# Two tiles at a time in self-attention, other orders in cross attention, and a last addition in two parts

## What is computed

```python
x = x + xattn(layernorm(x), ctx, mask)     # x 32x32x1024, ctx 32x257x1024: scores against the
                                           # context itself, softmax, weighted sum of the context
x = x + attn(layernorm(x), Wq, Wk, Wv, Wo) # 16 heads of 64, causal over the 32 positions of a batch row
x = x + ffn(x, w_gate, w_up, w_down)       # silu(x @ w_gate.T) * (x @ w_up.T), then @ w_down.T; 4096 hidden
```

## Time and profile before

| | us |
|---|---|
| median of 3 runs | 1494.79 |
| lowest, highest | 1493.11, 1496.1 |
| the profiled execution | 1494.51 |
| its span, first to last instruction | 1492.7 |
| PE busy | 1471.3 |
| POOL, DVE, ACT busy | 870.1, 764.6, 550.3 |
| one looped group of self-attention | 100.87 |
| one chunk of the feed-forward loop | 57.47 |

### The profile page before, as it was taken

How to read it: one execution, slowest core, us unless ns; L and a number is a source line. 1 busy time by engine, 2 the same in 40 slices (tenths; PEclk the granted TensorE clock), 3 DMA queues, 4 the chain that set the end, 5 groups by cost and what they waited for, 6 DMA issues and landing times.

```text
span 1492.7 us, 23122 instructions
## 1 busy us (share of the span) xinstructions
PE 1471.3 (99%) x7940; PEld 1197.3 (80%) x7940; DVE 764.6 (51%) x1229; ACT 550.3 (37%) x1090; POOL 870.1 (58%) x709
## 2 busy tenths in 40 slices
PE   7899999999999999999999999999999999999998
PEld 5666888887888888888888888888888888888886
DVE  4777154162361587843634625626626526436446
ACT  4457232132231354334334334344343433443442
POOL 1224211302212121579779789789788798798795
PEclk9999999999999999999999999999999999999999
DMA  9895200101101000112112111121121121121123
GB/s 380 336 382 212 113 29 29 56 28 56 56 27 58 1 1 22 38 51 74 35 56 64 44 61 56 49 63 50 56 63 49 55 65 49 42 77 30 55 63 112
DMA packets 43382, 117.35 MB, mean 79 GB/s; under 512 B 4944, under 2 KB 5200, under 8 KB 40528
## 3 DMA queue, kind: packets, MB, share of 16 engines
q1 hardware_dynamic: 42912, 116.44, 22.4%
q10 hardware_dynamic: 432, 0.39, 0.1%
HBM read 112.62 MB, written 4.19 MB: 78 GB/s over the span
## 4 chain that ended last, share of the span: by engine, by line
PE 94%; DVE 3%; DMA 1%; issue 1%; ACT 1%; SPq 0%; POOL 0%; DVEq 0%; ACTq 0%; POOLq 0%
PE ps L1318 38%; PE ps L1338 18%; PE ps L968 9%; PE ps L970 9%; PE ps L969 9%; PE ps L1005 3%; PE ps L1026 2%; PE ps L1048 2%; PE ps L974 1%; PE ps L1119 1%; PE ps L1162 1%; DMA cT<-in_turned 1%; DVE x L1745 1%; DMA ctx<-in_ctx 0%; DVE att L1531 0%
## 5 line engine op out<-in xcount | busy, mean ns | idle before, releaser
L583 POOL TENSOR_TENSOR b_lo<-blk,b_hi 128x512 fp32r<-128x512 f32 x180 | 231.8, 1296 | 49.2 <-ACT b_hi L863 38.9
L1745 DVE TENSOR_TENSOR x<-ps,x 128x1024 f32<-128x1024 f32 x210 | 242.1, 1210 | 0.0
L494 POOL TENSOR_TENSOR w_lo<-raw,w_hi 128x2048 fp32r<-128x2048 f32 x16 | 73.6, 4600 | 274.9 <-ACT w_hi L705 274.9
L1318 PE MATMUL ps<-xT_hi,b_hi 128*128 128x512 f32 x480 | 186.7, 389 | 0.0
L1318 PE MATMUL ps<-xT_lo,b_hi 128*128 128x512 f32 x480 | 186.7, 389 | 0.0
L1318 PE MATMUL ps<-xT_hi,b_lo 128*128 128x512 f32 x480 | 186.7, 389 | 0.0
L1338 PE MATMUL ps<-b_hi,b_hi 128*128 128x512 f32 x420 | 166.4, 396 | 0.0
L1338 PE MATMUL ps<-b_lo,b_hi 128*128 128x512 f32 x420 | 163.7, 390 | 0.0
L1338 PE MATMUL ps<-b_hi,b_lo 128*128 128x512 f32 x420 | 163.5, 389 | 0.0
L1719 DVE TENSOR_TENSOR hid<-ps,kept 128x512 f32<-128x512 f32 x60 | 41.5, 692 | 233.7 <-PE ps L1318 193.8
L583 POOL TENSOR_TENSOR b_lo<-s_sum,b_hi 128x512 fp32r<-128x512 f32 x105 | 136.4, 1299 | 35.8 <-ACT b_hi L863 35.8
(11 more groups left out here) (155 smaller groups left out, 3206.9 us busy)
## 6 DMA issues: line engine op xcount, KB each, us to landing
blk<-in_blocks SPq DMA_DIRECT2D x180, 256.0 KB, 2.7
ctx<-in_ctx SPq DMA_DIRECT2D x64, 512.0 KB, 10.7
raw<-in_w SPq DMA_DIRECT2D x19, 1024.0 KB, 4.8
x<-in_x SPq DMA_DIRECT2D x8, 512.0 KB, 7.0
ext_row<-in_ext SPq DMA_DIRECT2D x8, 512.0 KB, 14.7
out<-x SPq DMA_DIRECT2D x16, 256.0 KB, 2.6
cT<-in_turned SPq DMA_DIRECT2D x3, 1032.0 KB, 9.4
mask<-in_mask ACTq DMA_DIRECT2D x1, 224.9 KB, 6.2
```

Source lines behind the costliest of these rows:

```text
L494: pool.tensor_tensor(w_lo[wslot][:, :], raw[slot][:, :], w_hi[wslot][:, :].bitcast(F32), ALU.subtract).then_inc(split_done[slot], 1)
L583: pool.tensor_tensor(b_lo[slot][:, :], src[:, :], b_hi[slot][:, :].bitcast(F32), ALU.subtract).then_inc(block_lo, 1)
L1318: mm = pe.matmul(ps[:, bank, :], stat[a], moving[b], start=first and m == 0, stop=(s == 3 and m == 2), skip_group_check=True)
L1745: dve.tensor_tensor(part, ps[:, bank:bank + 2, :], part, ALU.add).then_inc(down_added, 1)
```

## The change

It has these parts:

- Groups 0 to 2: values, scores and attend are issued for two tiles at a time, the odd tile in the upper half of the bank (`tile_cols`); values of tiles 2 and 3 go to bank 2. ACT, DVE: one instruction for both tiles where one can be (copies, maximum, reciprocal, product, transposes, low parts), with buffers of two tiles in one tensor, and `oT` for four tiles. The projections of odd tiles go to banks 2 and 3.
- All four groups: the wait for `k_kept` stands ahead of the first values; DVE adds both halves of a projection in one instruction; `wo_done` and `wo_free` count in twos. The last group keeps its order, with tile t in the half `t % 2`.
- Start: x's tile 0 is issued after one context block; PE makes 12 transposes of the identity before the first context.
- Tile 1: DVE's copy for `context(1, 3)` moves ahead of `next_normalise(2)`.
- Last tiles: the turn of tile 7 goes to banks 2 and 3, with the waits that these need; `row_hi(3)` on ACT moves behind the last probabilities, `add_readout(7)` on DVE ahead of `row_lo(4)`, `turn_rows(6)` on PE behind the first query job.
- Feed-forward: the last addition of a chunk (place 6, second half) is made in two instructions of one tile, the first as soon as its own matmuls are done (`third_done`).

```diff
@@ cross attention, SP, ACT
             for b in range(BT):
                 context(0, 0, b).then_inc(first_full[0][b], 16)
-            sync.dma_start(x[:, 0, :], x_in[:, 0, :]).then_inc(x_full[0], 16)
+                if b == 0:
+                    sync.dma_start(x[:, 0, :], x_in[:, 0, :]).then_inc(x_full[0], 16)
...
             exps(NT - 1)
-            row_hi(3)
             probabilities(NT - 1)
             weigh_extra(NT - 1)
+            row_hi(3)
+            row_normalise(5)
             row_hi(4)
-            row_normalise(5)
             row_normalise(6)
@@ cross attention, PE, DVE
             def next_turn(t):
                 pe.wait_ge(next_ready, t + 1)
-                if t > 1:
+                if t == NT - 1:
+                    pe.wait_ge(c_act_done, act_before(t * KP))
+                    pe.wait_ge(c_dve_done, dve_before(t * KP))
+                elif t > 1:
                     pe.wait_ge(readout_free, t - 1)
-                if t == NT - 1:
-                    pe.wait_ge(xt_ready, 1)
-                turn(xn[0], RO).then_inc(next_psum, 1)
+                turn(xn[0], next_bank(t)).then_inc(next_psum, 1)
...
+            for i in range(WARM):
+                pe.transpose(ps[:, SC, 0:P], ident[:, :], ident[:, :])
             context(0, 0)
...
             job(Q_BANKS[0], 0, 0).then_inc(q_done, 1)
+            turn_rows(6)
             turn_rows(7)
...
                 if t + 2 < NT:
                     next_stats(t + 2)
+                    if t == 0:
+                        context(1, 3)
                     next_normalise(t + 2)
                 add_readout(t)
                 row_stats(t)
-                context(t + 1, 3)
+                if t:
+                    context(t + 1, 3)
...
             row_lo(3)
+            add_readout(NT - 1)
             row_lo(4)
-            add_readout(NT - 1)
@@ self-attention, PE, groups 0 to 2
+                pe.wait_ge(k_kept, g * 4 + 4)
+                if not last:
...
+                    def scores_pair(i):
+                        if i:
+                            pe.wait_ge(att_read, g * 8 + 2 * i)
+                        scores(g, 2 * i)
+                        scores(g, 2 * i + 1).then_inc(att_done, 2)
...
+                    def project_tile(t):
+                        if t == 0:
+                            pe.wait_ge(split_done[3], g + 1)
+                        pe.wait_ge(oT_ready, g * 8 + 2 * (t // 2 + 1))
+                        if t == 1:
+                            pe.wait_ge(v_kept, g * 8 + 4)
+                        elif t > 1:
+                            pe.wait_ge(wo_free, g * 16 + 2 * t)
+                        project(t, PROJECT_BANKS[t % 2])
+
+                    values_pair(0)
+                    scores_pair(0)
+                    values_pair(1)
+                    values_pair(2)
+                    scores_pair(1)
+                    attend_pair(0)
+                    values_pair(3)
+                    project_tile(0)
+                    scores_pair(2)
+                    attend_pair(1)
+                    project_tile(1)
+                    project_tile(2)
+                    project_tile(3)
+                    scores_pair(3)
+                    attend_pair(2)
+                    pe.wait_ge(att_read, (g + 1) * 8)
+                    pe.wait_ge(split_done[0], g + 2)
+                    job(0, 0, 0).then_inc(q_done, 1)
+                    project_tile(4)
+                    project_tile(5)
+                    attend_pair(3)
+                    job(1, 0, 1).then_inc(q_done, 1)
+                    project_tile(6)
+                    project_tile(7)
+                    return
@@ self-attention, ACT, groups 0 to 2
+                    keep_values_pair(0)
+                    exps_pair(0)
+                    keep_values_pair(1)
+                    keep_values_pair(2)
+                    keep_heads_pair(0)
+                    exps_pair(1)
+                    keep_values_pair(3)
+                    pair_split(g, 4)
+                    keep_heads_pair(1)
+                    exps_pair(2)
+                    keep_heads_pair(2)
+                    exps_pair(3)
+                    keep_queries(g + 1, 0)
+                    keep_heads_pair(3)
+                    keep_queries(g + 1, 1)
@@ self-attention, DVE, groups 0 to 2
+            def add_projected(g, t, bank=6):
+                dve.wait_ge(wo_done, g * 16 + 2 * (t + 1))
+                part = x[:, t, :].rearrange("p (e n) -> p e n", e=2)
+                dve.tensor_tensor(part, ps[:, bank:bank + 2, :], part, ALU.add).then_inc(wo_free, 2)
...
+                    for i in range(4):
+                        if i == 2:
+                            add_tile(0)
+                        mask_tile(2 * i)
+                        if i:
+                            heads_lo_pair(i - 1)
+                        mask_tile(2 * i + 1)
+                        tops_pair(i)
+                        if i == 2:
+                            add_tile(1)
+                        if i == 3:
+                            add_tile(3)
+                        turn_pair(i)
+                        if i == 2:
+                            add_tile(2)
+                    add_tile(4)
+                    add_tile(5)
+                    heads_lo_pair(3)
+                    add_tile(6)
+                    add_tile(7)
@@ feed-forward, DVE
+                if place == 6 and q == 1:
+                    half, col = ADD_TO[place]
+                    for i in (2, 3):
+                        if i == 2:
+                            dve.wait_ge(third_done, c)
+                        else:
+                            dve.wait_ge(pair_done, c * PAIRS)
+                        part = x[:, half * 4 + i, col * HALF:(col + 1) * HALF]
+                        dve.tensor_tensor(part, ps[:, DOWN_BANKS[place] + i, :], part, ALU.add)\
+                            .then_inc(down_added, 1)
+                    return
```

More of the change, by code:

```diff
@@ new lines, in attend, with project @@
+                def attend(t):
+                    for h in range(HG):
+                        r = slice((h % 2) * DK, (h % 2 + 1) * DK)
+                        at = t % 2 * FT * P + h // 2 * P
+                        mm = pe.matmul(ps[r, 4, at:at + P], v[:, t, h * DK:(h + 1) * DK],
+                                       att_z[t % 2][:, (h % 2) * 2 + h // 2, :], start=True, stop=True)
+                    return mm
+                def project(t, bank):
+                    for f in range(FT):
+                        for half in range(2):
+                            at = f * D + half * HALF
+                            mm = three(ps[:, bank + half, :], (oT_hi[t][:, f, :], oT_lo[t][:, f, :]),
+                                       (w_hi[1][:, at:at + HALF], w_lo[1][:, at:at + HALF]),
+                                       start=(f == 0), stop=(f == FT - 1))
+                    mm.then_inc(wo_done, 2)
@@ L1146, in values, with scores_one, attend_one @@
                         pe.wait_ge(v_kept, g * 8 + t)
-                    for k in range(KD):
-                        mm = three(ps[:, 5, 0:W], tokens(k, t * P, P),
-                                   (w_hi[0][:, k * W:(k + 1) * W], w_lo[0][:, k * W:(k + 1) * W]),
-                                   start=(k == 0), stop=(k == KD - 1))
-                    mm.then_inc(v_done, 1)
-                def attend(t):
+                    values(t, 5).then_inc(v_done, 1)
+                def scores_one(st):
+                    if st:
+                        pe.wait_ge(att_read, g * 8 + st)
+                    scores(g, st).then_inc(att_done, 1)
+                def attend_one(t):
                     pe.wait_ge(att_turned, g * 8 + (t + 1))
@@ L1159, in attend, with project_one @@
                         pe.wait_ge(oT_ready, g * 8 + t)
[L1160 to L1166 removed]
+                    attend(t).then_inc(pv_done, 1)
+                def project_one(t):
                     if t == 0:
@@ L1178, in project @@
-                    mm.then_inc(wo_done, 1)
-                values(0)
-                pe.wait_ge(k_kept, g * 4 + 4)
-                scores(g, 0)
-                values(1)
+                    pe.wait_ge(wo_free, g * 16 + (2 * t + 2))
+                    project(t, 6)
+                values_one(0)
+                scores_one(0)
+                values_one(1)
                 for st in range(1, NT):
-                    pe.wait_ge(att_read, g * 8 + st)
-                    scores(g, st)
+                    scores_one(st)
@@ L1190, in group @@
                     if st >= 2:
-                        attend(WITH_SCORES[st])
+                        attend_one(WITH_SCORES[st])
                     if st < NT - 1:
-                        values(st + 1)
+                        values_one(st + 1)
                     if st == 3:
-                        attend(2)
+                        attend_one(2)
                     if st >= 2:
```

(4 more changed lines are left out.)

274 lines of the change are left out of this document (160 added, 114 removed).

## The result

The kernel before takes 1494.79 us (the median of five executions, not of three as the table ahead has it), the changed kernel 1499.4 us (median of 5, 1497.44 to 1502.31): 1.0039 times as long, with a 95% interval of 1.0027 to 1.005. It is slower. The forecast was 1494.8 and no change; the time lies inside the range, near its high end, and the direction is missed. One later execution of the kernel before took 2229.89 at a granted clock of 0.616, and is in no ratio here.

A forecast was written before the change was run, and what follows sets the result against it. PE, busy 99% of the span, was taken as the bound. Terms -4.5 + 1.0 + 0 + 2.65 + 0.9 + 0 = +0.05 on the profiled 1494.51; with the median 0.28 above it, 1494.8. Range 1491.8 to 1500.0.

The forecast's parts named there:

- start: Kernel start: x issued earlier makes context row 3 land 1.3 later; loss taken as 1.0, 0.8 if warm-up brings full clock.
- cross attention, tile 1: Earlier DVE copy for batch row 3 shortens PE's 3.79 wait and half clock: -4.5, bounds -3.5 and -5.7.
- end of cross attention: Last tiles: no xT_lo wait -0.45, earlier pT copy -0.3, turn_rows(6) moved out of PE's wait +0.7; together 0.
- group 0 to 2, each: Looped self-attention groups: -2.85 gained, +1.0 and +2.73 in new waits; +0.88 each, +2.65 for three.
- last group: Last self-attention group: +1.0 for the k_kept wait, less 0.1 for merged DVE additions; +0.9.
- last addition: Kernel end: SP is still issuing stores, so an earlier half of the data gains 0, bounds -0.5 and +0.2.
- (a): Every group's start: PE waits for DVE's last K copy ahead of the first values, 1.0 lost each.
- (b): Groups 0 to 2: PE waits for att_read 8 before the next query job, idling 2.73; bounds 1.5 and 3.3.
- The pairing: Groups 0 to 2: fewer runs of heads and turns save 2.4, two wo_free waits 0.45; 2.85 a group.
- the case of 1.3: Start: the loss if the warm-up transposes don't bring full clock by the context row's transposes.
- likeliest case: Whole kernel: the forecast itself, 1492 to 1497.5, chance 0.52.
- Rival 1: Groups 0 to 2: idling 2.73 loses the clock, up to 3.4 a fall; 1498.2, 1501.6 or 1505; chance 0.27.

The follow-up runs named there:

- best1: Changed kernel with k_late's and reordered's edits, the old start, 96 bytes of padding ahead of oT, and DVE's addition of tile 2 behind the masks: 1482.71 us (0.9923).
- after: The changed kernel itself, with the whole change made to the kernel before: 1499.4 us (1.0039).
- tile1_copy: The kernel before with only DVE's copy of context part 3 of tile 1 moved ahead of the normalisation of tile 2: 1489.9 us (0.9974).
- reordered: Changed kernel with tile 3's projection behind scores 6 and 7, and DVE's low part of heads 4 and 5 behind masks and tile 3's addition: 1492.88 us (0.9993).
- place192: best1 with the oT buffers 128 bytes further on, at 192 modulo 256: 1483.44 us, one execution.
- place128: best1 with the oT buffers 64 bytes further on, at 128 modulo 256: 1482.46 us, one execution.
- oT_shifted: The kernel before with an unused tensor of 32 bytes a partition ahead of its oT buffers: 1494.77 us (1.0007).
- no_warm: Changed kernel without its 12 warm-up transposes: 1500.35 us (1.0048).
- after_again: The changed kernel run once more, unchanged: 1498.55 us (1.0033).
- aligned: Changed kernel with an unused tensor of 32 bytes a partition ahead of the oT buffers, so each starts at a multiple of 64 bytes: 1498.32 us (1.0026).
- k_late: Changed kernel with the wait for k_kept back behind the first values matmuls, in looped groups and the last: 1498.44 us (1.0029).
- best2: best1 with turn_rows(6) back ahead of the first query job and DVE's low part of tile 4 back ahead of its last readout addition: 1483.21 us (0.9927).

## Why the prediction was wrong, point by point

| step | forecast | profiled execution |
|---|---|---|
| start | +1.0 | +1.06 |
| cross attention, tile 1 | -4.5 | -4.8 |
| between tile 1 and the end | 0 | +0.3 |
| end of cross attention | 0 | +0.4 |
| group 0 to 2, each | +0.88 | +1.51 |
| last group | +0.9 | +1.3 |
| last addition | 0 | 0 |
| falls of the clock (median against profile) | 0.28 | 2.0 |

**What held.** (a), 0.94 for 1.0, and (b), 2.73 for 2.73, each read as a chain from PE's own last result. The pairing gives 2.57 in best1; 2.85 was forecast, and best1 has one run of heads more than after, which costs 0.19 + 0.20 - 0.15 = 0.24 by the forecast's own prices. Tile 1 gave 4.8, and tile1_copy alone 4.5. The start's 1.06 for 1.0 is partly luck: full clock is on record only from 14.31, which was the case of 1.3. The warm-up and the last addition are worth nothing: SP still issues its twelve last stores 0.6 apart, from 1485.68, with DVE done at 1491.4.

**What failed in the sum.** The forecast took the length of a matmul as fixed ("no matmul less"), and only counted edges and waits. That is the first step that failed. The step from start to start rose from 0.2286 to 0.234 in the projection. In full stretches that is 0.45 a group (reordered less best1 in the table, 23.04 less 22.59) and 0.17 in the last group, by the traces of the same two, 1.5 in all. It was in the diff: six small buffers became three, and oT moved by 96 bytes with them. place192 and place128, which differ in nothing but 64 bytes, and oT_shifted show it. A looped group missed its forecast by 0.63 (102.38, where 101.8 was to be seen); 0.2 of that stay unexplained, and as much in the last group.

**What failed in the likeliest case.** The forecast put the waits of 2.73 at their own length and nothing behind them; that is the second step that failed. Rival 1, with a chance of 0.27, had the mechanism. It asked whether a wait of 2.73 loses the clock or not; it does so in some executions. The profiles with this wait have a fall at none of three (after, no_warm), one (after_again), two (aligned) and three (k_late) of them, and of the twelve executions of after three stand at 0.999. In every one of these profiles a fall was 3.4 us at half and cost 1.2 to 1.5, not the 3.4 read off tile 1, where the half clock lasted 6.8. The 2.0 between the profiled execution and the median are worth 1.3 such falls; the executions that make the median have no trace, so that these were falls is inferred from their clocks and from reordered, where the waits and the spread went together. The section "HAM oscillation — how this bites in real kernels" of the Trainium skill's page "TensorE: Matmul & The Clock Gate" has the clock lost at every wait between bursts of matmuls, but its waits are of 3 to 5 us, longer than the 2.73 here, so the forecast's 1505 asked more of it than it states. At the waits of this case the clock was lost as that section has it in k_late's profile (three of three), and not in after's (none of three). Why one wait loses the clock and another doesn't is open.

**The end of cross attention.** Between tile 1 and the end, 0.3 are one wait for loaded context (111.63, 0.52 where the kernel before waited 0.20). The credits came (-0.65 for -0.75), but moving turn_rows(6) cost 1.08, not 0.7: PE waits 0.83 for the last addition, and the turn's 0.9 comes on top a job later. best2 did not get it back by the old order.

**The table adds up.** Measured less forecast, row by row: 0.06 - 0.3 + 0.3 + 0.4 + 3 x 0.63 + 0.4 + 1.7 = 4.5, of the 4.6 by which 1499.4 misses 1494.8. That 1499.4 lies inside the range is luck: the high end of 1500.0 stood for one fall of 3.4 or for a tile 1 that gains nothing, and neither came at that price.

## What to carry to other kernels

Pairing small work on PE is worth its edges (2.6 us a group here), but every wait that the pairing moves together must be costed as a chain from PE's own last result, with DVE's whole queue ahead of it; and where one such wait is covered, look at once for what stands behind it (reordered, best2). Where a change adds, merges or drops SBUF buffers, compare the places of matmul operands before and after: here the pace of the fp32r matmuls of 512 columns hangs on them (other forms were not varied). And read a wait that may lose the clock as a share of executions, not as yes or no.

## What the runs showed of the hardware that was not expected

- The step of fp32r matmuls of 512 columns, at full clock and with PE busy throughout, goes from 0.2267 to 0.234 us with the places of the stationary and the moving operand in SBUF; mostly their distance counts (equal modulo 256: fastest, in the projection). In the FFN 64 bytes of shift between the two operands made 0.2267 to 0.2333, and the same shift of both left it at 0.227 in the median. No rule for all distances was found, and no cause. The Trainium skill's page "SBUF — State Buffer", section "Operand start alignment", asks for a start at a multiple of the element's size and says "This is about legality, not speed"; every start here is a multiple of 32 bytes, and the traces show that the speed still differs by 3%.
- An idle time of 2.7 on PE, three times an execution, lost the clock at none of them in one profile of the changed kernel and at one in another, and at all three in k_late; waits of 1.05 and less in self-attention did so in none of the profiles. Each of these falls had 3.4 us at 0.50 in the records and cost 1.2 to 1.5.
- The wait of 3.79 in tile 1 of the kernel before had 6.8 us at 0.50 in its profile, from 41.04 on, 0.94 ahead of the wait's end; in that of oT_shifted (3.80) it had 3.4, from 42.98 on, 1.2 behind it. With the shorter one the first group of self-attention began 1.4 earlier.
